# Attention and routed experts on one core: indices scattered a step later, statistics three tiles ahead, half of the W13 low parts made on TensorE, the last group ranked before the first gate

## The chip, the core and the metric

The kernel runs on one core of a Trainium2 chip. A core has TensorE (matmuls, result in PSUM banks of 512 fp32 columns), VectorE, ScalarE and GpSimd, which work beside each other and wait for each other by semaphores, and SyncE, which here only issues DMAs. The metric is the device time of one execution in microseconds.

## The reference

`x` is 4 x 512 x 512. The first layer adds a masked cross attention whose values are the normalised rows of x weighted element by element, the second a mixture of eight experts of which each token uses two.

```
xn = layernorm(x)                                     # (4, 512, 512)
scores = (ctx @ Wq.T + bq) @ (ctx @ Wk.T + bk).T * 128**-0.5 * xn
x = x + tanh(g_xattn) * softmax(where(mask, -inf, scores))
xn = layernorm(x)                                     # 2048 tokens of 512
w = sigmoid(xn @ Wg.T);  top 2 of 8 by w + bias, weights normalised to 1
x = x + tanh(g_ffn) * sum_e w_e * ((silu(xn @ W1[e].T) * (xn @ W3[e].T)) @ W2[e].T)
```

## The kernel before

**First half: 16 steps, one for each tile of 128 tokens.** Step s does the following for tile s, with parts of the neighbouring tiles between. TensorE computes the scores of the next tile (L889, fp32, two records in the trace) and its masks (L897, L898), transposes the normed rows of the tile before (L911) and computes the logits of the tile before that (L921). Every fourth step it projects q and k of the next batch (L882) into the banks `ps_q` and `ps_k`. In most steps it also runs twice three matmuls whose result nobody reads (`spin`, L904). VectorE multiplies scores with x (L658), takes the row maximum (L662), computes the bias of the exponential (L669), the statistics of the tile two further on (`first_stats`, L649 to L653) and, after the exponentials, the residual sum (L681). ScalarE takes the exponentials (L520), the sum of squares (L526), and copies the transposed rows (L535). GpSimd computes reciprocal square roots (`row_scales`, L389) and the normed rows (L404).

**Splitting the weights.** Matmuls of the experts run in fp32r; for precision each weight is split into a high part (a rounded copy) and a low part (weight minus high part). W13 comes in 16 units of 128x1024 (two for each expert), W2 in 8. In step s ScalarE makes the high parts of `SPLITS[s]` units (L558); the low part is made one step later by GpSimd for the units in `LO_BY_POOL` (L409) and by VectorE for the rest (L820). The low part is written over the weight as it was loaded. `LOADS` says in which step ScalarE issues the load of which weights.

**Routing.** Tiles are routed in groups of 6, 4 and 6. When a group's logits are there, VectorE ranks the experts of each token (`router_ranks`, L701 to L715), makes weights (`router_weights`, L724 to L735), and, when TensorE has counted positions (L931 to L940), the indices (`router_slots`, L750 to L762). GpSimd scatters each tile's entries, two DMAs for a tile, to a table of slots in DRAM (`enter_slots`, L416): `SCATTERS` gives for a step its group and the range of DMAs; the entries of group 0 begin in step 8, in which VectorE makes their indices. GpSimd works strictly in order: row scales, normed row, low parts, scatters. `list_tiles` makes the list of expert tiles: 13 entries after ten tiles are routed, the others after all 16.

**Second half: 39 list tiles.** For list tile i SyncE loads 128 slots (L334), GpSimd gathers their normed rows (L431, three buffers `xg`), TensorE transposes them (L959), ScalarE and VectorE split them (L572, L799), TensorE multiplies with W13 (`hidden`, L971 to L973), ScalarE and VectorE compute the gate (L580, L805, L808), TensorE transposes it (L983), VectorE splits it (L814, L816), TensorE multiplies with W2 (`output`, L999 to L1001), ScalarE scales the rows (L591) and GpSimd adds them to the output in DRAM (L450, an accumulating indirect DMA, called store below). Two buffers `y` hold the scaled rows. Stores 0 to 2 each wait until the one before has landed; later ones do so where `list_landed` asks for it, that is, where the expert changes. The 12 scatters of the last group stand between these stores (`LATE_SCATTERS`: before store i-1 in round i). The third gather waits for the logits of tile 15, because the columns they read lie in its buffer.

The order of all instructions is written out by hand in one program for each engine, and each engine works it off in order.

## Time and profile before

| | |
|---|---|
| median of 3 runs | 350.77 us (350.27 to 351.55) |
| the profiled execution | 353.24 us, its span in the trace 351.50 us |
| busy share of the span | TensorE 82%, VectorE 55%, ScalarE 36%, GpSimd 56% |
| bytes moved | 48.69 MB, mean 139 GB/s |
| median landing of an x tile's load | 4.4 us |
| median landing of a slot scatter | 7.4 us |
| chain that ended last, by engine | DMA 28%, issue 25%, GpSimd 17%, TensorE 15%, VectorE 10% |

The shares are means over two different halves: in the page's 40 slices of 8.8 us TensorE is at 9 tenths in nearly every slice from the 23rd on, while slices 7 to 15 vary. So it is read by stage, with the timeline: each row of it has the start, the duration, the engine and line, and in brackets how long the engine stood idle before it and what ended that.

### The profile page before, as it was taken

What the parts mean: (1) busy time and instruction counts of PE and PEld (TensorE: products, weight loads), DVE (VectorE), ACT (ScalarE), POOL (GpSimd) and SP (SyncE); (2) the same over time, 40 slices, a digit from 0 to 9 for tenths busy, and PEclk for the clock granted to TensorE, in tenths of its full rate; (3) what the DMA queues carried; (4) which work ended last, traced back from release to release, by engine and by line L of the source; (5) the groups of instructions that cost most, each with busy time, mean ns of one, the idle gap of its engine ahead of it and who ended that gap; (6) DMA issues with size and microseconds to landing.
All of it is one profiled execution on the core that took longest, in us unless ns stands there. A gap on an engine that the chain in (4) does not pass through costs nothing.

```text
span 351.5 us, 5188 instructions
## 1 busy us (share of the span) xinstructions
PE 289.7 (82%) x1324; PEld 210.3 (60%) x1330; DVE 193.0 (55%) x493; ACT 128.2 (36%) x239; POOL 197.7 (56%) x193
## 2 busy tenths in 40 slices
PE   3888985967787335898759899999999999999981
PEld 1244542534344224786547788888888888888860
DVE  3597989884999312775223445445545444544530
ACT  2677772644336322221113133332233333233320
POOL 4099794688568442237774555455545544754313
PEclk9999998588858558899969899999999999999996
DMA  7997978375884023335799556666556664865444
GB/s 203 334 408 269 340 234 340 122 174 91 282 200 90 3 61 101 110 62 60 50 74 118 79 105 121 103 122 108 109 100 121 122 98 84 144 107 113 58 61 60
DMA packets 27026, 48.69 MB, mean 139 GB/s; under 512 B 9524, under 2 KB 10296, under 8 KB 25976
## 3 DMA queue, kind: packets, MB, share of 16 engines
q0 software_dynamic: 9760, 20.49, 36.3%
q1 hardware_dynamic: 14408, 15.04, 14.3%
q10 hardware_dynamic: 2832, 12.85, 11.8%
q8 instruction: 13, 0.21, 0.3%
q14 instruction: 13, 0.11, 0.1%
HBM read 28.51 MB, written 19.85 MB: 138 GB/s over the span
## 4 chain that ended last, share of the span: by engine, by line
DMA 28%; issue 25%; POOL 17%; PE 15%; DVE 10%; POOLq 2%; ACT 2%; SPq 0%; ACTq 0%; DVEq 0%
DMA out<-rows,slot 23%; POOL slot_table L416 5%; POOL rows L431 5%; POOL out L450 3%; PE bank L882 3%; DMA rows<-xn_rows,slot 2%; PE bank L889 2%; PE bank L904 2%; PE bank L921 2%; DVE rows L681 1%; POOLq L442 1%; DMA w_hi<-in_ctx_t 1%; PE bank L911 1%; PE bank L959 1%; POOL rstds L389 1%
## 5 line engine op out<-in xcount | busy, mean ns | idle before, releaser
L450 POOL DMA_INDIRECT out<-rows,slot x39 | 62.2, 1596 | 77.0 <-DMA out<-rows,slot 33.8
L799 DVE TENSOR_TENSOR xt_lo<-bank,xt_hi 128x512 fp32r<-128x512 f32 x39 | 27.0, 691 | 75.9 <-ACT xt_hi L572 75.9
L971 PE MATMUL bank<-w_hi,xt_hi 128*128 x156 | 66.5, 427 | 0.0
L973 PE MATMUL bank<-w_hi,xt_lo 128*128 x156 | 62.3, 399 | 0.0
L972 PE MATMUL bank<-w_lo,xt_hi 128*128 x156 | 61.9, 397 | 0.0
L431 POOL DMA_INDIRECT rows<-xn_rows,slot x39 | 40.0, 1025 | 27.0 <-issue 16.8
L416 POOL DMA_INDIRECT slot_table<-entry,slot_index x32 | 35.4, 1105 | 24.3 <-DVE slot_index L762 16.0
L591 ACT ACTIVATE rows<-bank,slot 128x512 f32<-128x512 f32 x39 | 26.8, 687 | 60.8 <-PE bank L1001 38.1
L580 ACT ACTIVATE rows<-bank 128x256 f32<-128x256 f32 x39 | 15.0, 384 | 81.8 <-PE bank L973 81.8
L999 PE MATMUL bank<-w_hi,gt_hi 128*128 x78 | 31.3, 402 | 9.8 <-DVE gt_lo L816 9.8
L805 DVE SCALAR_TENSOR_TENSOR rows<-rows,bank 128x256 f32<-128x256 f32 x39 | 16.3, 419 | 37.9 <-ACT rows L580 37.8
L959 PE MATMUL bank<-ident,rows 128*128 128x128 f32 x156 | 25.7, 291 | 11.3 <-DMA rows<-xn_rows,slot 11.3
L973 PEld LDWEIGHTS bank<-w_hi,xt_lo 128*128 128x128 f32 x156 | 30.0, 192 | 7.0
L971 PEld LDWEIGHTS bank<-w_hi,xt_hi 128*128 128x128 f32 x156 | 30.6, 196 | 5.3 <-issue 0.4
L972 PEld LDWEIGHTS bank<-w_lo,xt_hi 128*128 128x128 f32 x156 | 30.6, 196 | 5.2
L1001 PE MATMUL bank<-w_hi,gt_lo 128*128 x78 | 31.2, 400 | 0.0
L1000 PE MATMUL bank<-w_lo,gt_hi 128*128 x78 | 30.8, 395 | 0.0
L959 PEld LDWEIGHTS bank<-ident,rows 128*128 128x128 f32 x156 | 20.9, 150 | 16.5 <-DMA rows<-xn_rows,slot 11.5
L904 PE MATMUL bank<-w_hi,ident_bf 128*128 128x512 bf16 x81 | 26.9, 449 | 2.9 <-ACT w_hi L515 2.6
L558 ACT CAST w_hi<-w_lo 128x1024 fp32r<-128x1024 f32 x24 | 24.3, 1036 | 9.7 <-DMA xn_rows<-w_hi 6.6
L572 ACT CAST xt_hi<-bank 128x512 fp32r<-128x512 f32 x39 | 22.6, 578 | 9.3 <-PE bank L959 9.3
L409 POOL TENSOR_TENSOR w_lo<-w_lo,w_hi 128x1024 fp32r<-128x1024 f32 x10 | 23.7, 2368 | 0.0
(128 smaller groups left out, 450.7 us busy)
## 6 DMA issues: line engine op xcount, KB each, us to landing
w_lo<-in_w ACTq DMA_DIRECT2D x8, 1024.0 KB, 6.8
xn_rows<-w_hi SPq DMA_DIRECT2D x17, 256.0 KB, 5.7
rows<-in_x SPq DMA_DIRECT2D x16, 256.0 KB, 4.4
out<-rows SPq DMA_DIRECT2D x16, 256.0 KB, 5.0
w_lo<-in_w ACTq DMA_DIRECT2D x8, 512.0 KB, 7.8
w_hi<-in_ctx_t SPq DMA_DIRECT2D x4, 256.0 KB, 4.3
slot<-slot_table SPq DMA_DIRECT2D x39, 1.0 KB, 1.7
rows<-xn_rows,slot POOLq DMA_INDIRECT x39, 4.2
```

Source lines behind the costliest of these rows:

```text
L416: pool.indirect_dma_start(out=table[:, :], out_offset=bass.IndirectOffsetOnAxis(ap=slot_index[:, g % 2, t, c:c + 1], axis=0), in_=entry[:, ...
L431: pool.indirect_dma_start(out=xg[:, i % XG, :], out_offset=None, in_=xn_rows[0:SPARE + P * READY[segment(i)], :], in_offset=bass.IndirectO ...
L450: pool.indirect_dma_start(out=out[0:SPARE + P * READY[segment(i)], :], out_offset=bass.IndirectOffsetOnAxis(ap=slot[:, i, 0:1].bitcast(U32 ...
L799: dve.tensor_tensor(xt_lo[:, i % 2].rearrange("p k s -> p (k s)"), ps_x[i % 2][:], xt_hi[:, i % 2].rearrange("p k s -> p (k s)").bitcast(F32),
L904: pe.matmul(ps_q[:], ident_bf[:], attn_neg[:, 0, :], start=True, stop=True)
L959: mm = pe.transpose(ps_x[i % 2][:, k * P:(k + 1) * P], xg[:, i % XG, k * P:(k + 1) * P], ident[:])
L971: pe.matmul(ps_h[i % 2][:], xt_hi[:, i % 2, k, :], hi, start=(k == 0), stop=False)
L972: pe.matmul(ps_h[i % 2][:], xt_hi[:, i % 2, k, :], lo, start=False, stop=False)
L973: mm = pe.matmul(ps_h[i % 2][:], xt_lo[:, i % 2, k, :], hi, start=False, stop=(k == KC - 1))
L999: pe.matmul(ps_o[i % 2][:], gt_hi[:, cols], hi, start=(c == 0), stop=False)
L1000: pe.matmul(ps_o[i % 2][:], gt_hi[:, cols], lo, start=False, stop=False)
L1001: mm = pe.matmul(ps_o[i % 2][:], gt_lo[:, cols], hi, start=False, stop=(c == FC - 1))
```

## The change

Numbers of lines are those of the kernel before. Seven things are changed.

- `LO_BY_PE`: in steps 3, 4, 6, 8, 9, 10, 11 and 12 TensorE makes the low part of one W13 unit: for each half of 512 columns, identity times the weight plus minus identity times the high part, into `ps_q` and `ps_k`; ScalarE copies both to the low part (`copy_lo`). VectorE makes no low part of W13 any more, GpSimd eight instead of ten, the last in step 8.
- `spin` runs five matmuls once a step instead of twice three, and not in the steps of `LO_BY_PE`.
- `SPLITS` and `LOADS` are shifted to fit.
- `SCATTERS` begins in step 9 and takes four DMAs in steps 13 and 14; `LATE_SCATTERS` begins in round 1, with two DMAs a round to round 5 and one in rounds 6 and 7.
- The first statistics of a tile, and its first row scale, come one step earlier, three tiles ahead.
- The columns of tile 15 lie in another row buffer, so the third gather does not wait for its logits. SyncE loads the first four slots before the store of tile 15's rows and the others behind it.
- In the second half the ranks of the last group stand before the first gate, its weights before the first split of the gate, its indices behind that. TensorE goes from hidden(0) through the last logits to hidden(1) and does the first gate's transposes behind it.

```diff
-    SPLITS = (1, 1, 2, 1, 2, 1, 2, 1, 2, 1, 2, 1, 1, 1, 1, 2)
-    LO_BY_POOL = (0, 1, 2, 4, 5, 7, 8, 10, 12, 14)
-    SCATTERS = {8: (0, 0, 3), 9: (0, 3, 6), 10: (0, 6, 9), 11: (0, 9, 12), 12: (1, 0, 2), 13: (1, 2, 5), 14: (1, 5, 8)}
-    LATE_SCATTERS = {2: (2, 0, 2), 3: (2, 2, 5), 4: (2, 5, 8), 5: (2, 8, 10), 6: (2, 10, 12)}
-    SPINS = 3
+    SPLITS = (1, 1, 2, 2, 1, 2, 1, 2, 1, 1, 1, 2, 1, 1, 1, 2)
+    LO_BY_POOL = (0, 1, 2, 4, 6, 7, 9, 10)
+    LO_BY_PE = {3: 3, 4: 5, 6: 8, 8: 11, 9: 12, 10: 13, 11: 14, 12: 15}
+    SCATTERS = {9: (0, 0, 3), 10: (0, 3, 6), 11: (0, 6, 9), 12: (0, 9, 12), 13: (1, 0, 4), 14: (1, 4, 8)}
+    LATE_SCATTERS = {1: (2, 0, 2), 2: (2, 2, 4), 3: (2, 4, 6), 4: (2, 6, 8), 5: (2, 8, 10), 6: (2, 10, 11), 7: (2, 11, 12)}
+    SPINS = 5
...
+            def subtract_high(step, projected):
+                unit = LO_BY_PE[step]
+                pe.wait_ge(s_hi, unit + 1)
                 pe.wait_ge(s_qk, 2 * projected)
+                pe.wait_ge(s_lo_act, 2 * sum(before_ < step for before_ in LO_BY_PE))
+                for c, bank_ in enumerate((ps_q, ps_k)):
+                    cols = slice(c * D, (c + 1) * D)
+                    pe.matmul(bank_[:], ident[:], raw(unit)[:, cols], start=True, stop=False)
+                    pe.matmul(bank_[:], minus_ident, high(unit)[:, cols], start=False, stop=True).then_inc(s_diff, 1)
...
+            def copy_lo(step):
+                for c, bank_ in enumerate((ps_q, ps_k)):
+                    n = 2 * sum(before_ < step for before_ in LO_BY_PE) + c
+                    act.wait_ge(s_diff, n + 1)
+                    act.copy(low(LO_BY_PE[step])[:, c * D:(c + 1) * D], bank_[:]).then_inc(s_lo_act, 1)
...
                 for unit in units_in(step):
                     split_hi(unit)
+                if step in LO_BY_PE:
+                    copy_lo(step)
                 squares(step)
...
                     row_done(TILES - XR + i)
-                    if i == 2:
-                        pool.wait_ge(s_logits, TILES)
...
-                if step + 2 < TILES:
-                    first_stats(step + 2)
+                if step + 3 < TILES:
+                    first_stats(step + 3)
...
             last = len(GROUPS) - 1
+            router_ranks(last)
             for i in range(LIST):
                 gate_rows(i)
                 if i + 2 < LIST:
                     gathered_lo(i + 2)
+                if i == 0:
+                    router_weights(last)
                 gated_transposed(i)
                 if i == 0:
-                    router_ranks(last)
+                    router_slots(last)
                 elif i == 1:
-                    router_weights(last)
-                elif i == 2:
-                    router_slots(last)
-                elif i == 3:
                     list_tiles(1)
...
                 if i == 0:
                     logits(TILES - 1)
+                    gathered(2)
+                elif i == 1:
+                    gate_transpose(0)
+                    positions(len(GROUPS) - 1)
+                    gathered(3)
+                    output(0, last)
+                    gate_transpose(1)
                 else:
                     output(i - 1, last)
-                if i + 2 < LIST:
-                    gathered(i + 2)
-                if i == 1:
-                    positions(len(GROUPS) - 1)
-                gate_transpose(i)
+                    if i + 2 < LIST:
+                        gathered(i + 2)
+                    gate_transpose(i)
```

TensorE before, in step 3, from the logits of tile 1 to those of tile 2: scores (L889), masks (L897, L898), spins (L904), transposes (L911), spins, logits (L921).

```order
L921 MATMUL bank<-wg_sb,w_hi 128x8 x4
L889 MATMUL bank<-w_hi 128x512
L897 MATMUL bank<-w_hi,ident_bf 128x512
L898 MATMUL bank<-w_hi,ident_bf 128x512
L904 MATMUL bank<-w_hi,ident_bf 128x512 x3
L911 MATMUL bank<-ident,w_hi 128x128 x4
L904 MATMUL bank<-w_hi,ident_bf 128x512 x3
L921 MATMUL bank<-wg_sb,w_hi 128x8 x4
```

TensorE in the changed kernel, same place. Scores are L912 there, the subtraction L931 and L932, masks L920 and L921, transposes L945, logits L955.

```order
L955 MATMUL bank<-wg_sb,w_hi 128x8 x4
L912 MATMUL bank<-w_hi 128x512
L931 MATMUL bank<-w_lo,ident 128x512
L932 MATMUL bank<-w_hi,gt_hi 128x512
L931 MATMUL bank<-w_lo,ident 128x512
L932 MATMUL bank<-w_hi,gt_hi 128x512
L920 MATMUL bank<-w_hi,ident_bf 128x512
L921 MATMUL bank<-w_hi,ident_bf 128x512
L945 MATMUL bank<-ident,w_hi 128x128 x4
L955 MATMUL bank<-wg_sb,w_hi 128x8 x4
```

Four matmuls on 512 columns stand where six spins were, and ahead of the masks.

GpSimd before, steps 8 and 9: row scales (L383, L389), normed row (L404), low part (L409), scatters (L416).

```order
L383 TENSOR_SCALAR variances<-sqsum 128x1
L389 TENSOR_TENSOR rstds<-variances,minus_half 128x2
L404 TENSOR_SCALAR w_hi<-rows,nmean,rstds 128x512
L409 TENSOR_TENSOR w_lo<-w_lo,w_hi 128x1024
L416 DMA slot_table<-entry,slot_index 19328x2 x3
L383 TENSOR_SCALAR variances<-sqsum 128x1
L389 TENSOR_TENSOR rstds<-variances,minus_half 128x2
L404 TENSOR_SCALAR w_hi<-rows,nmean,rstds 128x512
L409 TENSOR_TENSOR w_lo<-w_lo,w_hi 128x1024
L416 DMA slot_table<-entry,slot_index 19328x2 x3
```

GpSimd in the changed kernel, same steps, in its own line numbers (row scales L394 and L400, normed row L415, low part L420, scatters L427).

```order
L394 TENSOR_SCALAR variances<-sqsum 128x1
L400 TENSOR_TENSOR rstds<-variances,minus_half 128x2
L415 TENSOR_SCALAR w_hi<-rows,nmean,rstds 128x512
L420 TENSOR_TENSOR w_lo<-w_lo,w_hi 128x1024
L394 TENSOR_SCALAR variances<-sqsum 128x1
L400 TENSOR_TENSOR rstds<-variances,minus_half 128x2
L415 TENSOR_SCALAR w_hi<-rows,nmean,rstds 128x512
L427 DMA slot_table<-entry,slot_index 19328x2 x3
```

Step 8 has no scatters any more and step 9 no low part.

GpSimd at the start of the second half, before: gathers (L431), then in round 2 the first two late scatters (L416) before store 1 (L450).

```order
L431 DMA rows<-xn_rows,slot 128x512 x4
L450 DMA out<-rows,slot 1536x512
L431 DMA rows<-xn_rows,slot 128x512
L416 DMA slot_table<-entry,slot_index 19328x2 x2
L450 DMA out<-rows,slot 1536x512
L431 DMA rows<-xn_rows,slot 128x512
L416 DMA slot_table<-entry,slot_index 19328x2 x3
```

In the changed kernel (gathers L440, scatters L427, stores L459):

```order
L440 DMA rows<-xn_rows,slot 128x512 x4
L427 DMA slot_table<-entry,slot_index 19328x2 x2
L459 DMA out<-rows,slot 1536x512
L440 DMA rows<-xn_rows,slot 128x512
L427 DMA slot_table<-entry,slot_index 19328x2 x2
L459 DMA out<-rows,slot 1536x512
```

The first two scatters stand before store 0, and no round has three.

## Rows read from the trace of the kernel before

**Rows 1.** The page, part 2: granted TensorE clock in 40 slices, tenths

```profile
PEclk9999998588858558899969899999999999999996
```

**Rows 2.** Groups by line: busy us, mean ns, idle us before

```profile
L416 POOL DMA_INDIRECT slot_table<-entry,slot_index x32 | 35.4, 1105 | 24.3 <-DVE slot_index L762 16.0 <-issue 7.7 <-PE bank L959 0.6
...
L558 ACT CAST w_hi<-w_lo 128x1024 fp32r<-128x1024 f32 x24 | 24.3, 1036 | 9.7 <-DMA xn_rows<-w_hi 6.6 <-PE bank L921 2.0 <-PE bank L889 0.9
L409 POOL TENSOR_TENSOR w_lo<-w_lo,w_hi 128x1024 fp32r<-128x1024 f32 x10 | 23.7, 2368 | 0.0
...
L520 ACT ACTIVATE bank<-w_hi,nbias,rstds 128x512 f32<-128x512 f32 x16 | 12.5, 781 | 20.5 <-DVE nbias L669 19.7 <-issue 0.6
...
L526 ACT ACTIVATE bank<-rows,nmean 128x512 f32<-128x512 f32 x16 | 11.0, 688 | 7.8 <-DVE nmean L684 7.8
...
L535 ACT COPY w_hi<-bank 128x512 f32<-128x512 f32 x15 | 8.7, 580 | 14.7 <-PE bank L911 14.5
```

**Rows 3.** Timeline of TensorE, first half: start, duration, line, idle before

```profile
33.48 1.06 PE L921 MATMUL bank<-wg_sb,w_hi 128*128 128x8 f32 x8
34.40 1.10 PE L889 MATMUL bank<-w_hi 128*128 128x512 f32 x2
...
38.81 1.10 PE L889 MATMUL bank<-w_hi 128*128 128x512 f32 x2
...
54.45 1.10 PE L889 MATMUL bank<-w_hi 128*128 128x512 f32 x2
59.87 0.61 PE L897 MATMUL bank<-w_hi,ident_bf 128*128 128x512 bf16 x1 [4.32 <-DVE zmax L662]
...
66.31 2.05 PE L889 MATMUL bank<-w_hi 128*128 128x512 f32 x2
...
93.74 0.61 PE L897 MATMUL bank<-w_hi,ident_bf 128*128 128x512 bf16 x1 [1.96 <-DVE zmax L662]
...
100.71 2.05 PE L889 MATMUL bank<-w_hi 128*128 128x512 f32 x2
...
109.28 1.10 PE L889 MATMUL bank<-w_hi 128*128 128x512 f32 x2
```

**Rows 4.** Timeline of VectorE: after group 0's weights, and group 1's first rank instruction

```profile
58.35 0.74 DVE L658 SCALAR_TENSOR_TENSOR w_hi<-rows,mv,bank 128x512 f32<-128x512 f32 x1
...
86.88 1.47 DVE L701 TENSOR_SCALAR sig<-sig 128x32 f32<-128x32 f32 x1
```

**Rows 5.** Timeline of GpSimd: first and last scatter of the first half

```profile
63.43 1.25 POOL L416 DMA_INDIRECT slot_table<-entry,slot_index  x1 [6.68 <-DVE slot_index L762]
...
114.96 0.96 POOL L416 DMA_INDIRECT slot_table<-entry,slot_index  x1 [0.30 <-issue]
```

**Rows 6.** Timeline of all engines, 149 to 198 us

```profile
149.90 1.64 POOL L450 DMA_INDIRECT out<-rows,slot  x1 [5.41 <-issue]
...
153.98 0.47 PE L971 MATMUL bank<-w_hi,xt_hi 128*128 x1
...
158.74 0.47 PE L971 MATMUL bank<-w_hi,xt_hi 128*128 x1
...
160.16 1.61 POOL L450 DMA_INDIRECT out<-rows,slot  x1 [0.30 <-issue]
...
180.39 1.61 POOL L450 DMA_INDIRECT out<-rows,slot  x1 [0.30 <-issue]
...
197.32 0.78 PE L971 MATMUL bank<-w_hi,xt_hi 128*128 x1
```

**Rows 7.** Timeline of all engines, 120 to 145 us

```profile
122.65 13.97 SPq L334 DMA_DIRECT2D slot<-slot_table  x13
...
131.65 0.79 PE L971 MATMUL bank<-w_hi,xt_hi 128*128 x1
...
137.52 1.08 POOL L431 DMA_INDIRECT rows<-xn_rows,slot  x1 [8.05 <-PE bank L921]
...
141.68 1.12 PE L959 MATMUL bank<-ident,rows 128*128 128x128 f32 x4 [4.95 <-DMA rows<-xn_rows,slot]
```

**Rows 8.** The chain that ended last: start, us, what

```profile
167.55 8.65 DMA out<-rows,slot
...
337.71 4.69 DMA out<-rows,slot
```

74 lines of the change are left out of this document (47 added, 27 removed).

## The prediction, made before the changed kernel was run

> **What bounds the kernel now.** I read the page's clock row, then the timeline of TensorE, then of the engines it waits for. The kernel has two halves. In the first, 16 steps, one per tile of 128 tokens, do attention and normalisation; in the second, 39 list tiles go through the experts. From list tile 9 on TensorE is never idle and a tile takes 4.76 us (153.98 to 158.74) [rows 6]; nothing in the change alters a tile there, so the 154 us from its tile 9 (197.32) [rows 6] to the end move as a block. All that can move the end lies before 197.32.
>
> In the first half a plain step is TensorE's own: from one scores to the next 34.40 to 38.81, 4.41 us, with no wait [rows 3]. Then it breaks. At 59.87 TensorE has waited 4.32 us for VectorE's row maximum, because the ranks and weights of group 0 stood in front of it on VectorE until 58.35 [rows 3, 4]. After each such wait the clock row shows the lower level, 1.2 GHz [rows 1], and a scores matmul pair takes 2.05 us [rows 3] where 2 x 0.47 is usual. Then GpSimd binds: the first scatter waits 6.68 us for its indices, and from there to the last scatter's end (114.96 + 0.96 = 115.92) it is nearly all scatters, row scales, normed rows and low parts [rows 5]. Scores(9), (10), (14) and (15) come at 54.45, 66.31, 100.71 and 109.28 [rows 3]: six steps in 55 us.
>
> In the passage to the second half, SyncE starts the slot loads at 122.65, 6.7 us after the last scatter, the first expert matmul starts at 131.65, and then TensorE idles 4.95 us for the third gather, which GpSimd issued only at 137.52, after waiting for the last logits [rows 7]. From tile 0 to tile 9 it needs 65.7 us, where nine tiles at 4.76 would be 42.8: 22.8 us are lost, in the end to accumulating stores that queue behind each other and behind twelve late scatters [rows 6].
>
> **The change, part by part**, in the profiled execution's time (353.24, span 351.50; the median of the runs is 350.77, 2.47 less, and I carry the difference over).
>
> *Low parts on TensorE.* Eight of 16 W13 low parts become two pairs of matmuls into the q and k banks plus two ScalarE copies. No row has this operation whole, but its pieces have: an identity matmul on 512 fp32 columns is like scores, two records of 0.47 at the high clock, and one in fp32r is 0.23, since a tile has 18 of them in its 4.76 us beside 0.6 of transposes. So 2 x (0.94 + 0.23) = 2.3 us on TensorE, and 2 x 0.58 on ScalarE (a copy of 128x512 from a bank takes 580 ns [rows 2]). It is not hidden by either engine, since the two form a ring: logits 0.92 (33.48 to 34.40), scores 0.94, subtraction 2.3, second copy 0.68 with its wait, squares 0.69 + 0.19, copy of the transposed rows 0.58, semaphores 0.25 in all, and the next logits wait for that copy. 6.5 us, against 4.41 [rows 2, 3]. From below, TensorE's own work in such a step is 5.3 us (no spins); from above, the same ring at 1.2 GHz is 0.92 + 0.94 + 2.3 more, 10.7. I take 6.5.
> What goes: six VectorE subtractions and, net, two GpSimd ones of 2.37 [rows 2].
>
> *Spins.* Six a step become five, and none in a low-part step: a plain step keeps its 4.4, since ScalarE with two units has 0.97 + 2 x 1.0 + 0.88 + 0.58 = 4.4 [rows 2]. In project steps nothing stands any more behind the wait for ScalarE's bias: 1.2 us less in step 2.
>
> Steps 2 to 7: step 2 -1.2, steps 3 and 4 +2.1 each, step 6 (low part and projection, about 7.1 against 6.8) +0.3: **+3.3**.
>
> *Step 8*, scores(9) to scores(10), 54.45 to 66.31, 11.9 us. Ranks end as before, 3.9 us after scores(9); then maximum and bias 1.7, exponentials 0.97, high part 1.04, two copies 1.2, squares 0.9, transposed copy 0.6, logits 0.95, waits 0.3: 11.4. **-0.5**. The low part fills most of the old 4.3 us wait, but the chain now runs over ScalarE.
>
> *Scatters a step later, statistics a tile earlier.* GpSimd no longer stands before normed rows waiting for indices, and the row scale of a tile no longer comes from behind that step's scatters. With no low part left in steps 9 to 14 its step is row scales and normed row 2.1 and three scatters 3.9 (1.1 each, 1.28 with the gap [rows 2]), 6.0: under the ring's 6.5. So steps 9 and 10 take 6.5 and 7.1; steps 11 and 12, with the ranks of group 1 between (4.1: the old 5.3, less the 1.3 by which their first instruction, 1.47 instead of 0.18, waited beside a GpSimd low part [rows 4]), 13.7; step 13 4.6. Scores(10) to scores(15): 31.9, before 109.28 - 66.31 = 43.0. **-11.1**. Behind that steps 13 and 14 have four scatters, and the last one ends 8.3 us after scores(15), before 6.6: **+1.7**. What is late next is ScalarE's chain, then GpSimd's four-scatter steps.
> The statistics ask for each x tile a step sooner. Tile 6 is issued at 24.36 and would be wanted about 27.6, with 4.4 us as the median landing: up to 1.2 us or, with the slowest landing (6.5), 3.3 of VectorE's waiting in step 3, and as much in steps 4, 6 and 7. The longer low-part steps cover it (+2.1 each); I count 0, at most 3.
>
> *Clock.* TensorE will still idle some 2 us in front of the maximum of step 8 and 3 more behind its transposes. Idle spells of 4.32 and 1.96 us were followed by the low level [rows 3, 1]; spells of about 1 us in the early steps were not. Bounds: 0, or one ring step and the rest of step 8 low, 4.2 + 0.7. I take **+2**.
>
> *SP.* One normed store goes ahead of the first slot load: **+0.4**. The first half so yields 3.3 - 0.5 - 11.1 + 1.7 + 2 + 0.4 = **-4.2** at the first expert matmul: 127.4.
>
> *Second half, up to tile 9* (in the old times, tile 0 at 131.65). The third gather needs no last logits and lands before 135, so tile 1 starts near 137.2 instead of 142.87. But VectorE now does the 3.2 us of ranks before the first gate, 137.0 to 140.2, then gate 0.9, weights 1.8, split 0.8: output(0) waits until 144.4, and tile 3 comes at 152.0 instead of 153.98. What matters is the stores: indices at 145.2 instead of 157.3, two scatters, store 0 at 148.0 (149.90), store 1 after store 0's landing (6.6 to 8.7 us [rows 8]) at 155 to 157 (160.16), store 2 at 162 to 165 (167.55). Then GpSimd's round is gather 1.3, two scatters 2.6, store 1.9: 5.8 instead of 7.1; store 4 at 174 to 177 (180.39). Tile 9 followed it by 16.9 us: 191 to 194 [rows 6]. **-6**, bounds -2 (only the two us at tile 3) and -12 (landing as fast as the later 4.7).
>
> Sum: 353.24 - 4.2 - 6 = 343.0, in the runs' terms 350.77 - 10.2 = **340.5**.
>
> On the stores the rows show landings of 8.65 us amid scatters and 4.69 later [rows 8]. The Trainium skill, "DMA: Bandwidth & Descriptors", section "Issuing engines are not separate DMA queues", says that all issuers share 16 engines and interleave; it goes against the gain, since spreading twelve scatters over seven rounds instead of five puts more stores beside them. By it the last term would be nearer its -2, and the sum 344.5.
>
> **Rivals.**
> 1. *The clock stays low through the ring* (slower). TensorE idles 1.2 us in every low-part step. At 1.2 GHz the ring gains 4.2 us a step. If steps 8 to 12 are all low, that is 5 x 4.2 = 21, less the 2 counted: 350.77 - 10.2 + 19 = 359.5. It decides from three such steps on (3 x 4.2 - 2 = 10.6). For it: after 59.87 and 93.74 the clock stayed low some 13 us [rows 1, 3]. Against it: TensorE works 5.3 us of 6.5, and in the first 50 us waits of 1.0 left the clock up. The Trainium skill's "TensorE: Matmul & The Clock Gate", section "A second HAM failure mode: psum-queue depth-cycling", tells of frequent short idles that make the clock oscillate; the ring would be such a case, and no row before shows it.
> 2. *The stores keep the second half* (less gain). Tile 9 waits for store landings; if these lengthen with gathers and scatters closer together, the six us there are nil and only the first half counts: 350.77 - 4.2 = 346.5. For it: 33.8 us of GpSimd's waits are on stores. Against it: the chain begins earlier in any case.
> 3. *Both run well* (more gain): no clock loss (-2), landings of 6.6 (-5): 333.5. For it: the low part fills the very idle time after which the clock fell.
>
> **How the numbers follow.** Forecast 0.52, rival 2 0.20, rival 3 0.17, rival 1 0.11. 0.5% or 1.75 us is about what a measurement tells from no change. Slower by more: rival 1's larger part, 0.09, and 0.01 of mishaps; within: 0.06, from rival 2's upper end (x tiles late, +3) and rival 1 with two low steps; faster: 0.84. The range leaves rival 1 and the best fifth of rival 3 out: 331.5 to 350. The likeliest's own is 336 to 345.
>
> **What would show it.** Low-part steps of 6.5 us between scores in steps 3, 4, 9 and 10; no wait of GpSimd for indices in step 9; the last scatter of the first half ending near 111; first expert matmul near 127; no gap before tile 1 but one of about 3 us before output(0); store 4 some 42 to 45 us after tile 0 instead of 48.7 (180.39 - 131.65). I am wrong if scores lie over 9 us apart in steps 9 and 10 (clock or x tiles), or if tile 9 still comes 65 us after tile 0.

## The result, and the profile after

The changed kernel takes **349.37 us** (median of 20 runs, 343.74 to 353.38), the kernel before 351.19 in the same series (20 runs, 348.71 to 353.74). The ratio is **0.9887, interval 0.9852 to 0.9923**, faster by 1.1% or 4 us, where 10 were forecast. Ratios and intervals in this document use only the executions within 1.5% of their kernel's fastest, which are all 20 of the kernel before but 7 of the 20 of the changed one, so its ratio flatters it: the medians of all executions lie 1.8 us or 0.5% apart (0.9948). The profiled execution took 348.12 us, its span is 346.4.

| stretch, profiled executions | forecast | before | after | difference |
|---|---|---|---|---|
| start to scores(9) | +3.3 | 54.45 | 59.00 | +4.6 |
| scores(9) to scores(10) | -0.5 | 11.86 | 12.00 | +0.1 |
| scores(10) to scores(15) | -11.1, clock +2 | 42.97 | 40.18 | -2.8 |
| scores(15) to the end of the last scatter | +1.7 | 6.64 | 8.98 | +2.3 |
| from there to the first expert matmul | +0.4 | 15.73 | 15.58 | -0.2 |
| **first expert matmul** | **-4.2** | 131.65 | 135.74 | **+4.1** |
| tile 0 to tile 9 | -6 | 65.67 | 57.20 | -8.5 |
| tile 9 to the end of the span | 0 | 154.18 | 153.46 | -0.7 |

The sum, -5.1, is the difference of the two profiled executions (353.24 and 348.12). The first is 2.05 us above its kernel's median and the second 1.25 below, so some 3 us of the table are a matter of which executions were profiled.

The groups by line, answering to [rows 2], with the new subtraction (L931) and copies (L609):

```profile
L427 POOL DMA_INDIRECT slot_table<-entry,slot_index x32 | 33.7, 1052 | 21.8 <-issue 14.7 <-DVE slot_index L781 6.9 <-ACT rows L603 0.3
...
L420 POOL TENSOR_TENSOR w_lo<-w_lo,w_hi 128x1024 fp32r<-128x1024 f32 x8 | 18.9, 2358 | 0.0
...
L931 PE MATMUL bank<-w_lo,ident 128*128 128x512 f32 x32 | 18.4, 660 | 0.0
...
L609 ACT CAST w_lo<-bank 128x512 fp32r<-128x512 f32 x16 | 9.2, 585 | 10.8 <-PE bank L932 10.8
```

Scatters wait less for indices than before, but 14.7 us "issue", for nothing that the profile can name. That is the new item. A copy takes 585 ns, as forecast. The records of the subtraction's identity matmul (two for each) average 660 ns; some ran at the low clock.

TensorE, first half, answering to [rows 3], with the page's clock row:

```profile
59.00 1.10 PE L912 MATMUL bank<-w_hi 128*128 128x512 f32 x2
...
71.00 2.05 PE L912 MATMUL bank<-w_hi 128*128 128x512 f32 x2
...
79.30 1.10 PE L912 MATMUL bank<-w_hi 128*128 128x512 f32 x2
...
86.22 1.13 PE L912 MATMUL bank<-w_hi 128*128 128x512 f32 x2
...
92.36 1.81 PE L912 MATMUL bank<-w_hi 128*128 128x512 f32 x2
...
100.31 1.10 PE L912 MATMUL bank<-w_hi 128*128 128x512 f32 x2
...
104.53 0.61 PE L920 MATMUL bank<-w_hi,ident_bf 128*128 128x512 bf16 x1 [3.12 <-DVE zmax L681]
...
109.45 1.88 PE L955 MATMUL bank<-wg_sb,w_hi 128*128 128x8 f32 x8 [0.68 <-ACT w_hi L545]
...
111.18 2.05 PE L912 MATMUL bank<-w_hi 128*128 128x512 f32 x2
```

```profile
PEclk9998999769885555889998999999999999999997
```

```profile
66.00:74.00 8.00, 6.09 (x31) 4.14 (x29) 6.55 (x23) 5.06 (x11) 4.02 (x6) 0.50 0.60 197
```

Scores(10) at 71.00, scores(11) at 79.30: 8.3 us instead of the 6.5 forecast, since the clock stood at 1.2 GHz from 66 to 74 us (0.50 in the row of the window above: busy us of TensorE, its weight loads, VectorE, ScalarE, GpSimd, then the clock); the next steps take 6.9, 6.1 and 8.0. Then, from 100.31 to 111.18, one step takes **10.9** where 4.6 was forecast. TensorE waits 3.12 us for VectorE's maximum, its clock falls to 1.2 GHz in that time, and its logits take 1.88 us instead of 1.06 and its scores 2.05. There is one more fall, at the start of the low-part step 12: the scores at 92.36 took 1.81 us, and no wait of TensorE since 79 us had been over 0.78 us. The granted clock, in the last column but two:

```profile
79.00:92.00 13.00, 12.22 (x49) 6.62 (x50) 8.23 (x31) 9.84 (x20) 9.29 (x13) 1.00 0.86 150
93.00:95.50 2.50, 2.50 (x5) 1.01 (x3) 2.43 (x5) 0.98 (x3) 2.02 (x3) 0.50 1.32 316
```

VectorE in that step: first and last instruction of `list_tiles(0)`, and what stands behind them.

```profile
99.21 0.26 DVE L787 TENSOR_REDUCE n_tiles<-compared 1x8 f32<-1x128 f32 x1
...
102.81 0.15 DVE L813 TENSOR_TENSOR used<-used,taken 1x7 f32<-1x7 f32 x1
...
103.00 0.75 DVE L677 SCALAR_TENSOR_TENSOR w_hi<-rows,mv,bank 128x512 f32<-128x512 f32 x1
...
103.78 0.69 DVE L681 CUSTOM_DVE_ANT_0 w_hi<-w_hi,bank 128x512 f32<-128x512 f32 x1
```

The list of expert tiles takes 3.8 us (99.21 to 102.96) in sixteen tiny instructions, and only then comes the product whose maximum TensorE waits for. The forecast had counted ranks and weights of group 1 but not this list.

GpSimd, answering to [rows 5]: second, third and last scatter of group 1.

```profile
102.49 0.96 POOL L427 DMA_INDIRECT slot_table<-entry,slot_index  x1 [0.30 <-issue]
...
110.05 0.97 POOL L427 DMA_INDIRECT slot_table<-entry,slot_index  x1 [6.60 <-issue]
...
118.82 1.34 POOL L427 DMA_INDIRECT slot_table<-entry,slot_index  x1 [0.30 <-issue]
```

Between two scatters of one step GpSimd stands for 6.60 us, and no engine and no DMA is named. Normed rows, TensorE's transposes of them and the last scatter all come behind that: the last scatter ends at 120.16, before at 115.92.

The second half, answering to [rows 6, 7] (SyncE's queue, TensorE and GpSimd):

```profile
135.74 0.79 PE L1005 MATMUL bank<-w_hi,xt_hi 128*128 x1
...
149.27 0.49 PE L1032 MATMUL bank<-w_hi,gt_hi 128*128 x1 [1.84 <-DVE gt_lo L837]
...
150.75 1.00 POOL L427 DMA_INDIRECT slot_table<-entry,slot_index  x1 [6.87 <-DVE slot_index L781]
...
153.34 1.63 POOL L459 DMA_INDIRECT out<-rows,slot  x1 [0.30 <-issue]
...
160.28 1.61 POOL L459 DMA_INDIRECT out<-rows,slot  x1 [1.43 <-DMA out<-rows,slot]
...
178.60 1.61 POOL L459 DMA_INDIRECT out<-rows,slot  x1 [0.30 <-issue]
...
192.94 0.48 PE L1005 MATMUL bank<-w_hi,xt_hi 128*128 x1
```

Here the forecast holds. There is no gap before tile 1 any more, and before output(0) TensorE waits 1.21 and 1.84 us, where one gap of 3 was forecast. Counted from tile 0, the first late scatter starts at 15.0 us (forecast 13.6, before 25.9), store 0 comes at 17.6 (before 18.3), store 1 at 24.5 (before 28.5), store 4 at 42.9 (before 48.7; forecast 42 to 45), tile 9 at 57.2.

### The profile page after: what moved, and what is told of

The parts are those of the page before. It is cut to its first block, busy times and chain, and to the rows that moved or that the text cites. A ratio compares the mean times of both kernels' runs of the same rounds, so it can differ in the third digit from the quotient of the medians.

```text
span 346.4 us, 5203 instructions
## 1 busy us (share of the span) xinstructions
PE 294.9 (85%) x1320; PEld 213.1 (62%) x1324; DVE 183.8 (53%) x488; ACT 135.5 (39%) x255; POOL 184.6 (53%) x192
## 3 DMA queue, kind: packets, MB, share of 16 engines
q10 hardware_dynamic: 2832, 12.85, 13.6%
## 4 chain that ended last, share of the span: by engine, by line
DMA 36%; issue 24%; PE 16%; POOL 11%; DVE 6%; ACT 4%; POOLq 2%; ACTq 0%; SPq 0%; DVEq 0%
DMA out<-rows,slot 29%; POOL rows L440 4%; DMA xn_rows<-w_hi 4%; PE bank L912 3%; POOL out L459 3%; PE bank L931 3%; POOL slot_table L427 3%; PE bank L955 3%; PE bank L905 2%; ACT bank L536 1%; DMA rows<-xn_rows,slot 1%; DMA w_hi<-in_ctx_t 1%; POOLq L451 1%; PE bank L938 1%; DMA slot_table<-entry,slot_index 1%
## 5 line engine op out<-in xcount | busy, mean ns | idle before, releaser
L459 POOL DMA_INDIRECT out<-rows,slot x39 | 62.0, 1591 | 70.7 <-DMA out<-rows,slot 36.8
L1007 PE MATMUL bank<-w_hi,xt_lo 128*128 x156 | 62.2, 399 | 0.0
L440 POOL DMA_INDIRECT rows<-xn_rows,slot x39 | 39.0, 1001 | 24.0 <-issue 16.7
L427 POOL DMA_INDIRECT slot_table<-entry,slot_index x32 | 33.7, 1052 | 21.8 <-issue 14.7
L993 PE MATMUL bank<-ident,rows 128*128 128x128 f32 x156 | 24.9, 284 | 6.7 <-DMA rows<-xn_rows,slot 6.7
L955 PE MATMUL bank<-wg_sb,w_hi 128*128 128x8 f32 x120 | 18.8, 284 | 10.2 <-ACT w_hi L545 10.2
L993 PEld LDWEIGHTS bank<-ident,rows 128*128 128x128 f32 x156 | 20.1, 146 | 11.9 <-DMA rows<-xn_rows,slot 7.2
L955 PEld LDWEIGHTS bank<-wg_sb,w_hi 128*128 128x128 f32 x120 | 18.0, 228 | 15.1 <-ACT w_hi L545 13.7
```

The source lines that it names most:

```text
L427: pool.indirect_dma_start(out=table[:, :], out_offset=bass.IndirectOffsetOnAxis(ap=slot_index[:, g % 2, t, c:c + 1], axis=0), in_=entry[:, ...
L440: pool.indirect_dma_start(out=xg[:, i % XG, :], out_offset=None, in_=xn_rows[0:SPARE + P * READY[segment(i)], :], in_offset=bass.IndirectO ...
L459: pool.indirect_dma_start(out=out[0:SPARE + P * READY[segment(i)], :], out_offset=bass.IndirectOffsetOnAxis(ap=slot[:, i, 0:1].bitcast(U32 ...
L955: mm = pe.matmul(ps_l[:, t * E:(t + 1) * E], normed_columns(tile)[:, k, :], wg_sb[:, k, :], start=(k == 0), stop=(k == KC - 1))
L993: mm = pe.transpose(ps_x[i % 2][:, k * P:(k + 1) * P], xg[:, i % XG, k * P:(k + 1) * P], ident[:])
L1007: mm = pe.matmul(ps_h[i % 2][:], xt_lo[:, i % 2, k, :], hi, start=False, stop=(k == KC - 1))
```

## The experiments

Twelve runs were made to find which part gains and which costs, six more on the wait that has no name. Each ratio is to the kernel before, run on the same chip in the same series; the series are on different chips, so a comparison of two kernels goes by their ratios and not by their times. Tile 0 stands for the first expert matmul.

| kernel | ratio [interval] | unnamed wait of a scatter, us | last scatter ends | tile 0 |
|---|---|---|---|---|
| changed | 0.9887 [0.9852, 0.9923] | 6.60, at the 15th | 120.2 | 135.7 |
| e1 room halved (two executions) | 1.0223 [1.0182, 1.0264] | 11.06 at the 8th, 4.22 at the 15th, 3.98 at the 20th | 129.8 | 143.4 |
| e2 list later | 0.9896 [0.9843, 0.9949] | 3.60, 15th | 121.1 | 137.1 |
| e3 second half only | 0.9839 [0.9801, 0.9876] | none | 115.6 | 131.3 |
| e4 first half only | 1.0196 [1.0168, 1.0225] | 3.32, 15th | 118.4 | 133.2 |
| e5 without TensorE's low parts | 0.9867 [0.9811, 0.9924] | 7.66, 15th | 119.1 | 133.6 |
| e6 e3 + statistics | 0.9787 [0.9731, 0.9843] | none | 117.4 | 133.1 |
| e7 e3 + new SCATTERS | 0.9821 [0.9753, 0.9889] | 8.55, 15th | 122.6 | 137.5 |
| e8 e3 + TensorE's low parts | 0.9768 [0.9719, 0.9817] | none | 119.8 | 135.4 |
| e9 changed, old SCATTERS | **0.9784 [0.9744, 0.9823]** | none | 117.9 | 133.2 |
| e10 three a step | 0.9935 [0.9891, 0.9978] | 5.36, 15th | 124.3 | 140.0 |
| e11 e9 + list later | **0.9764 [0.9726, 0.9802]** | none | 120.8 | 136.7 |
| e12 e3, old late scatters | 0.9859 [0.9813, 0.9905] | none | 115.8 | 132.3 |
| e13 e9, W2 loads earlier | 0.9827 [0.9785, 0.9868] | none | 118.4 | 134.8 |
| e14 small x1 stores | 0.9866 [0.9803, 0.9928] | 8.47, 15th | 123.1 | 137.8 |
| e15 W2 loads earlier | 0.9953 [0.9907, 0.9998] | 7.03, 15th | 123.0 | 138.1 |
| e16 room for twelve | 0.9934 [0.9889, 0.9978] | 6.57, at the 13th | 122.7 | 138.0 |
| e17 e9, room for twelve | 0.9846 [0.9801, 0.9892] | 8.21, at the 13th | 118.5 | 133.5 |
| e18 two first | 1.0027 [0.9996, 1.0058] | none | 124.2 | 140.0 |

The last three columns are from one execution each. Executions of one kernel differ by 2.8% or more (343.74 to 353.38 for the changed one), so a tile 0 that is 2 us off says little by itself; the ratios decide.

**e1, room for descriptors.**

```diff
-SCRATCH = 2048
+SCRATCH = 1024
```

> The changed kernel with the descriptor buffer of GpSimd's DMAs halved (1024 instead of 2048). In step 13 GpSimd stood 6.6 us between its second and third scatter with no releaser in the trace. Theory R (room for descriptors): it waited for older scatters to give their room back; with half the room such waits come at many scatters, gathers and stores and the kernel is slower by 10 us or more. Rival (the wait has another cause, and room is not short): the time stays within 1 us of the changed kernel's, 349.

```profile
98.69 0.97 POOL L427 DMA_INDIRECT slot_table<-entry,slot_index  x1 [11.06 <-issue]
```

The wait grows to 11.06 us and two more appear; 1.0223 is 3.4% over the changed kernel's ratio (2.7% by the medians of all executions), from two executions. The unnamed wait has to do with the room for GpSimd's descriptors: nothing else was changed.

**e2, the list out of step 13.**

```diff
-                    if END[g] in READY:
-                        list_tiles(READY.index(END[g]))
...
+            list_tiles(0)
             for unit in units_in(TILES - 1):
                 split_lo(unit)
```

> The changed kernel, with the list of the first 13 expert tiles made by VectorE after the last residual sum instead of in step 12, where its 3.7 us stand before the row maximum of tile 13. Theory V (VectorE): that block idles TensorE 3.1 us, the clock falls and step 13 takes 10.9 us; without it scores(14) to scores(15) take 5 to 6 us, the first half ends 3 to 5 us earlier, and the time is 345 to 346. Rival G (GpSimd): its 6.6 us wait in step 13 sets the end of the scatters by itself; step 13 gets shorter on TensorE but the last scatter still ends near 120 and the time stays at 349.

The step becomes 6.9 us instead of 10.9, and the time stays (0.9896). So TensorE's and VectorE's loss in step 13 isn't what the end waits for; in the profile the last scatter still ends at 121.1, with an unnamed wait of 3.60 us before it.

**e3 and e4, one half each.** e3 has the first half of the kernel before and the second of the changed one, e4 the reverse.

```diff
-    LO_BY_PE = {3: 3, 4: 5, 6: 8, 8: 11, 9: 12, 10: 13, 11: 14, 12: 15}
+    LO_BY_PE = {}
...
-    SCATTERS = {9: (0, 0, 3), 10: (0, 3, 6), 11: (0, 6, 9), 12: (0, 9, 12), 13: (1, 0, 4), 14: (1, 4, 8)}
+    SCATTERS = {8: (0, 0, 3), 9: (0, 3, 6), 10: (0, 6, 9), 11: (0, 9, 12), 12: (1, 0, 2), 13: (1, 2, 5), 14: (1, 5, 8)}
...
-            row_scales(-2)
...
-            first_stats(2)
```

> Only the second half of the change on the kernel before (ranks of the last group ahead of the first gate, late scatters from round 1, third gather without the last logits, slot loads split); the first half as before. Theory A (the halves add up): the first expert matmul stays near 131.7, tile 9 comes 57 us later, and the time is 342 to 343, 9 below the kernel before. Rival: the second half's gain needs the changed first half (DMAs of the first half landed by then), and the time is 346 to 349.

> Only the first half of the change (low parts on TensorE, scatters a step later, statistics three ahead), the second half as before. Theory A: the first expert matmul is at 135 to 136 and the time is 355, 4 above the kernel before. Rival: with the old second half the later start is partly taken up by its waits for stores, and the time is 351 to 352.

The second half alone brings 1.6%, or 5.6 us of 351, the six forecast. The first half alone costs 2.0%, or 6.9 us, where a gain of 4.2 was forecast. They don't add up to the changed kernel's -1.1%; the rest (about 5 us, or 2 to 3 by the medians of all executions) is not accounted for.

**e5 to e8, the first half's parts.** e5 is the changed kernel without TensorE's low parts; e6, e7 and e8 add to e3 the earlier statistics, the new SCATTERS, and TensorE's low parts (with `SPLITS`, `LOADS` and spins). As e3 against e7:

```diff
-    SCATTERS = {8: (0, 0, 3), 9: (0, 3, 6), 10: (0, 6, 9), 11: (0, 9, 12), 12: (1, 0, 2), 13: (1, 2, 5), 14: (1, 5, 8)}
+    SCATTERS = {9: (0, 0, 3), 10: (0, 3, 6), 11: (0, 6, 9), 12: (0, 9, 12), 13: (1, 0, 4), 14: (1, 4, 8)}
```

> The changed kernel without the low parts on TensorE: units, loads and spins of the first half as in the kernel before, but scatters from step 9 and statistics three tiles ahead, and the new second half. The new second half alone ran at 0.984 of the kernel before, the whole change at 0.989, the first half alone at 1.020. Theory P (the low parts on TensorE cost what is lost, by steps of 6.1 us and the ring over ScalarE): this runs at 0.975 to 0.985. Rival S (twenty scatters in six steps run out of descriptor room): it still waits for room in steps 12 to 14 and runs at 0.99 or more.

> The new second half alone plus statistics and row scales three tiles ahead. Theory P and rival S both expect the same as without it, 0.984, since the bias of the exponentials waited for row scales only 1.0 us in the kernel before; a third theory X (VectorE waits for x tiles that land late, as it does for 1.9 us in the changed kernel) expects 2 us more, 0.990.

> The new second half alone plus scatters from step 9, four each in steps 13 and 14. Rival S: waits without a releaser at the later scatters, the last one ends later than 115 and the time is 0.99 to 1.00. Theory P: GpSimd no longer stands 6.7 us before the first scatter, the last one ends earlier or at the same time, 0.975 to 0.985.

> The new second half alone plus the low parts on TensorE (with their units, loads and spins), scatters from step 8 as before. Theory P: low-part steps of 6.1 us instead of 4.4 put off the first scatters by 3 us and more, and the time is 0.99 to 1.00. Rival S: the low parts cost nothing at the end, since GpSimd's scatters bind as before, and with four GpSimd low parts fewer the time is 0.98.

TensorE's low parts show no cost in the time: 0.9768 against e3's 0.9839, though low-part steps take 6.1 us. Nor do the statistics (0.9787). So far the unnamed wait is in each kernel with the new SCATTERS and in none with the old. In the time this shows in one pair, 0.9867 (e5) against 0.9787 (e6), whose intervals still overlap, and not in the other (e7 against e3). So one run more:

**e9, the changed kernel with the old SCATTERS; e10, three a step; e11, e9 with the list later; e12, the spacing of the late scatters.**

```diff
+    SCATTERS = {8: (0, 0, 3), 9: (0, 3, 6), 10: (0, 6, 9), 11: (0, 9, 12), 12: (1, 0, 2), 13: (1, 2, 5), 14: (1, 5, 8)}      e9, e11
+    SCATTERS = {9: (0, 0, 3), 10: (0, 3, 6), 11: (0, 6, 9), 12: (0, 9, 12), 13: (1, 0, 3), 14: (1, 3, 6), 15: (1, 6, 8)}     e10
+    LATE_SCATTERS = {2: (2, 0, 2), 3: (2, 2, 5), 4: (2, 5, 8), 5: (2, 8, 10), 6: (2, 10, 12)}                               e12, on e3
```

> The changed kernel with one line back as it was: SCATTERS starts in step 8 and has three DMAs a step, two in step 12. Theory S (the new SCATTERS takes back what the rest gains): about 344 us, 0.977 of the kernel before, no wait without a releaser over 1 us among GpSimd's scatters, last scatter of the first half ending at 117 to 119. Theory A (low parts on TensorE and statistics three ahead lose only together, whatever the scatters do): 349 us as the changed kernel, 0.989, list tile 0 at 135 or later.

> The changed kernel with the scatters of group 1 spread as three, three and two over steps 13, 14 and 15, so the start in step 9 stays and no step has four. Theory F (the four in a row fill the room for descriptors): the wait of 6.6 us in step 13 shrinks to under 2, the last scatter ends at 117 to 119, about 346 us (0.983). Theory L (the later start does it, since as many descriptors must be moved in a shorter stretch beside the loads of W2): the wait of 4 to 8 us stays, somewhere in steps 12 to 15, last scatter at 120 or later, about 349 us (0.989).

> The changed kernel with the old SCATTERS and the first list of expert tiles behind the last residual, out of step 13. If VectorE's 3.8 us there count once GpSimd no longer binds: 341 us (0.971), 3 us under the same kernel with the list in its place. Rival G (GpSimd's scatters and row scales set the end of the first half in this form too): no difference from it, within 1 us of 344.

> The kernel with only the second half changed (344.67 us, 0.984) with the old spacing of the last group's scatters: from round 2, three a round in rounds 3 and 4. Theory D (the stores come sooner because fewer scatters stand between them): half of the gain goes, 347.5 us, 0.992, and list tile 9 comes 58 us after tile 0 instead of 54. Rival T (only the earlier ranks, indices and third gather count): within 1 us of 344.7, tile 9 at 54 to 55 us.

With the one line back, the ratio is 0.9784, its interval clear of the changed kernel's: the new SCATTERS costs 1.0%, or 3.6 us (1.6% by the medians of all executions). Three a step doesn't cure it (0.9935, wait 5.36): so it isn't the fours, and the later start is what is left. The list's place is again worth nothing that shows (e11 against e9). For e12 the answer stays open: 0.9859 against 0.9839 with overlapping intervals, though in its one profile tile 9 came 62.2 us after tile 0 instead of 54.0.

GpSimd in e9, the fourteenth and fifteenth scatter, and VectorE's subtraction beside the fifteenth:

```profile
103.87 0.96 POOL L427 DMA_INDIRECT slot_table<-entry,slot_index  x1 [0.30 <-issue]
...
107.13 1.22 DVE L841 TENSOR_TENSOR w_lo<-w_lo,w_hi 128x1024 fp32r<-128x1024 f32 x1
...
107.21 2.07 POOL L427 DMA_INDIRECT slot_table<-entry,slot_index  x1 [0.28 <-issue]
```

Row scales and a normed row stand between the two, so the fifteenth comes 3.3 us after the fourteenth without an unnamed wait. It takes 2.07 us instead of 0.96 to 1.09, but that is no sign of the room. A VectorE subtraction on 128x1024 (L841) had started 0.08 us before it, and every first-half scatter over 1.7 us in e9, the changed kernel and the kernel before stands beside such a subtraction: the 11th of the changed kernel (1.81 us), the 2nd, 4th, 15th and 19th of the kernel before (1.75 to 2.07). In e11 the fifteenth takes 1.06 and the fourteenth, with the subtraction beside it, 1.92.

**e13 to e15, is it the traffic?** Loads of W2 one step earlier, in e9 (e13) and in the changed kernel (e15); in e14 the stores of x1 are cut from tile 8 on, as its expectation says, so it leaves out 448 of 512 columns of these rows, and only its waits and its time are read.

```diff
-    LOADS = {..., 7: (7,), 8: (8,), 9: (9,), 10: (10, 11), 11: (12, 13), 12: (14, 15)}
+    LOADS = {..., 7: (7, 8), 8: (9,), 9: (10, 11), 10: (12, 13), 11: (14, 15)}                    e13, e15
...
-                sp.dma_start(out[SPARE + tile * P:SPARE + (tile + 1) * P, :], x_row(tile))
+                cols = D if tile < 8 else D // 8
+                sp.dma_start(out[SPARE + tile * P:SPARE + (tile + 1) * P, 0:cols], x_row(tile)[:, 0:cols])      e14
```

> The changed kernel with the old SCATTERS (345.34 us, 0.978) and the loads of W2 one step earlier each (steps 7 to 11 instead of 8 to 12). If the loads beside group 1's scatters still cost something there: 342 us (0.970) and the last scatter a us or two before 117.9. If not, or if the bytes only collide earlier with the stores of steps 8 and 9: 345 us (0.978), within 1.5 us.

> The changed kernel with the stores of x1 from tile 8 on cut to their first 64 of 512 columns (the rest of these rows isn't written; as many descriptors, 1.8 MB less to move, about 1.1 of them between 85 and 120 us). Theory T (bytes in flight beside the scatters delay their descriptors, so that the room stays full): the wait without a releaser in step 13 falls from 6.6 us to under 3, W2 loads land in under 12 us instead of 14. Theory N (only the number of descriptors and when they are issued counts): the wait stays at 5 to 8 us and the time within 1.5 us of the changed kernel's 349.4.

> The changed kernel, new SCATTERS included, with the loads of W2 one step earlier each. Theory T: two of the W2 loads no longer stand beside group 1's scatters, the wait of 6.6 us in step 13 falls to under 4 us, about 347 us (0.983). Theory N: the wait stays at 5 to 8 us and the time at 349.4 (0.989).

The wait is 8.47 us with 1.8 MB less to move and 7.03 with the loads moved. Theory T fell; both kernels with earlier loads are slower, if anything (e13 0.9827 against e9's 0.9784, e15 0.9953 against 0.9887).

**e16 to e18, the end of the ring.** In e18 group 1's scatters come as two, three and three.

```diff
-SCRATCH = 2048
+SCRATCH = 1792                                                                            e16, e17 (on e9)
...
+    SCATTERS = {..., 12: (0, 9, 12), 13: (1, 0, 2), 14: (1, 2, 5), 15: (1, 5, 8)}         e18
```

> The changed kernel with the room for descriptors at 1792 bytes instead of 2048. The long wait stood at the fifteenth scatter with 2048 and at the eighth with 1024, so a scatter takes between 137 and 146 bytes and twelve fit in 1792. Theory W (the room is a ring; the first scatter that doesn't fit in it waits until the ones before it have landed): the wait moves to the thirteenth scatter, the first of step 13, 3 to 7 us long, and the fifteenth has none; the last scatter comes 1 to 3 us sooner than 118.8, 347.5 us (0.985). Theory U (room for so many in flight, less room is worse): still a wait at the third and fourth scatter of step 13 as well, over 8 us in all, 352 us (1.00).

> The changed kernel with the old SCATTERS (345.34 us, 0.978) and room for twelve scatters. Theory W: the thirteenth scatter waits for its indices until 102.5 in any case, so the end of the ring costs nothing there, no wait without a releaser over 1 us comes up, and the fifteenth takes about 1.0 us instead of 2.07; last scatter 1 us sooner than 116.9, 344 us (0.975). Theory U: waits of some us at the thirteenth to eighteenth scatter, 348 us (0.987).

> The changed kernel with group 1's scatters as two, three and three in steps 13, 14 and 15, room as it was. Theory W: the fifteenth scatter is now the first of step 14 and stands behind its row scales and normed row, so the long wait stands there and is 1 to 4 us instead of 6.6 (5.36 with three, three and two); last scatter at 120 or later, since three come in step 15; 348 to 351 us. Theory U: no wait over 1 us, since never more than three are issued in a row.

GpSimd in e16, the twelfth, thirteenth and fifteenth scatter:

```profile
97.38 0.96 POOL L427 DMA_INDIRECT slot_table<-entry,slot_index  x1 [0.30 <-issue]
...
108.09 1.07 POOL L427 DMA_INDIRECT slot_table<-entry,slot_index  x1 [6.57 <-issue]
...
111.69 0.96 POOL L427 DMA_INDIRECT slot_table<-entry,slot_index  x1 [0.30 <-issue]
```

The wait has moved to the thirteenth, as theory W said, and the fifteenth has none. So the room is used up in order, like a ring: fourteen scatters fit in 2048 bytes, twelve in 1792, seven in 1024, and the one after them waits though the first ones landed long before.

What ends the wait can be read from the landings. The changed kernel's twelfth scatter (start 96.75, the last of group 0) and its fourteenth (102.49):

```profile
L427 POOL DMA_INDIRECT slot_table<-entry,slot_index x1: 958/958/958, 96.7 to 96.7; - x1
DMA to landing us min/median/max: 12.7/12.7/12.7
...
L427 POOL DMA_INDIRECT slot_table<-entry,slot_index x1: 958/958/958, 102.5 to 102.5; - x1
DMA to landing us min/median/max: 9.8/9.8/9.8
```

The twelfth landed at 109.4, and the fifteenth started 0.6 us later, at 110.05. The fourteenth landed at 112.3, after that: so the fifteenth doesn't wait for the one ahead of it. The same 0.6 to 0.7 us lie between the twelfth's landing and the fifteenth's start in e2 (110.6, 111.27), e4 (108.2, 108.92), e14 (111.3, 111.94) and e15 (111.8, 112.46), while over all kernels whose fifteenth waits with 2048 bytes it starts anything from 4.3 us (e4) to 9.9 (e7) after the scatter ahead. In e1 the eighth starts at 98.69 and the seventh landed at 98.1. In e16 the last landing of group 0 that the trace records is at 107.4, and the thirteenth starts at 108.09. Why it is the twelfth, of fourteen in the room, stays open.

This tells why starting a step sooner helps: in the kernel before the twelfth had landed at 101.8, 1.7 us before the fifteenth came up (103.55), and in e9 the last recorded landing of group 0 is at 102.4 and the fifteenth comes up at 107.2. What W said of the time fell: in e16 the last scatter ends at 122.7, no sooner, and 0.9934 isn't better than the changed kernel. The end of the wait is the same landing, and eight scatters instead of six are behind it. In e18 the fifteenth scatter, now behind a step's row scales, starts at 112.22 and has no wait at all, and yet that kernel is the slowest of all but e1 and e4: its scatters go on into step 15 and end at 124.2. e17's 8.21 us lie where e9 waits 5.99 for the indices, so most of them are that wait under another name (its thirteenth starts at 102.84, e9's at 102.48); its last scatter ends at 118.5, not sooner than e9's, and theory W's 344 us were 345.9. Moving the ring's end gave nothing; starting a step sooner did.

## Why the prediction was wrong

The first half's term failed: -4.2 us at the first expert matmul were forecast, +4.1 were measured in the profile, and the first half alone (e4) costs 2.0%. The forecast counted twenty scatters as engine time only and saw no wait behind them, and it left the list of expert tiles out of step 13. The second half's term held. Of the stretch forecast at -11.1 (scores(10) to scores(15), measured -2.8), step 13 missed 6.3 us and step 9 missed 1.8.

- **Low parts on TensorE.** Forecast 6.5 us for such a step, measured 6.1 at the high clock (30.23 to 36.31). To scores(9) +4.6 instead of +3.3. Mechanism right, and by e8 no cost of it shows in the time. The miss is beside the low-part steps: the 1.2 us of step 2 were not gained, since its five spins ran at the low clock (0.50 from 24.5 to 27.7 us, 2.31 us instead of 1.25), and the plain steps 5 and 7 took 4.9 us instead of 4.4.

```profile
24.40 2.31 PE L938 MATMUL bank<-w_hi,ident_bf 128*128 128x512 bf16 x5
```

- **Step 8, forecast -0.5, measured +0.1.** The terms written out for it add up to 11.6 us and not 11.4; measured 12.0.
- **The clock.** A low stretch behind the wait of step 8 was forecast at +2; step 9 took 8.3 instead of 6.5, +1.8. Three more weren't: in step 2, at 92.36 and in step 13. Rival 1, the low clock through the whole ring, didn't happen: steps 10 and 11 took 6.9 and 6.1. Behind that rival stood the Trainium skill's "TensorE: Matmul & The Clock Gate", section "A second HAM failure mode: psum-queue depth-cycling". In steps 3 and 4 the trace shows no such oscillation (1.00 from 29 to 60 us); the short fall at 92.36, behind low-part steps with waits of at most 0.8 us, may be of the kind that it tells of, and step 12, which begins with it, took 8.0 us.
- **Step 13, forecast 4.6, measured 10.9.** This is the largest error of a single step. "The ranks of group 1 between" were priced at 4.1; the 3.8 us of `list_tiles(0)` behind them were left out. In the kernel before the same list stood at the same place (VectorE, 98.45 to 101.78), and TensorE waited only 1.13 us for the maximum behind it. As soon as GpSimd's work was taken away, the next engine's own row had to be priced, and it wasn't. With the low clock behind it this makes the 6.3 us that step 13 missed. e2 shows that mending this alone gives nothing in the time.

```profile
103.89 0.60 PE L898 MATMUL bank<-w_hi,ident_bf 4*128 4x512 bf16 x1 [1.13 <-DVE zmax L662]
```

- **"Steps 13 and 14 have four scatters": +1.7, measured +2.3.** The price per scatter was right, the path wrong, and this is the step of the argument that the time turns on. The last scatter was to end near 111 and ended at 120.2. The end of the first half is the path from group 1's indices over eight scatters to the slot loads. From the first to the end of the last of these scatters before took 17.1 us (98.81 to 115.92), after 19.1 (101.10 to 120.16) with 6.6 of wait in it, e9 15.4 (102.48 to 117.88). The forecast counted scatters as engine time only. Their descriptors need room, and the fifteenth starts only after the landing of the twelfth. In the kernel before that landing came 1.7 us before the fifteenth scatter did, so the wait was just missed, and a later start brings it out. GpSimd's rows of the kernel before, the twelfth scatter with its landing (91.17 + 10.6 = 101.8) and the fifteenth:

```profile
L416 POOL DMA_INDIRECT slot_table<-entry,slot_index x1: 958/958/958, 91.2 to 91.2; - x1
DMA to landing us min/median/max: 10.6/10.6/10.6
...
103.55 2.07 POOL L416 DMA_INDIRECT slot_table<-entry,slot_index  x1 [0.28 <-issue]
```

- **Starting a step later.** The forecast took the wait of 6.68 us [rows 5] as lost, and its removal as a gain. But the first steps didn't gain from its removal what was forecast: scores(14) came at 100.31 instead of 100.71 before, where 98.4 was forecast with the clock's +2, and the indices of group 1 were ready no sooner (VectorE's last instruction for them ends at 99.3, before at 98.5). The later start puts the landing of group 0's scatters 7.6 us later (109.4 instead of 101.8), into the path that counts. e9 puts it at 1.0% of the time. With that mended the first half still has no gain: tile 0 comes at 133.2 in e9 and, with the list moved too, at 136.7 in e11. That part of the miss is laid to the clock and to step 2 from the trace alone; no run tests it.
- **Statistics three ahead** cost nothing, as counted.
- **Second half, forecast -6 (-2 to -12).** Measured -8.5 in the profile and 1.6% (5.6 us) by e3. Tile 3 gained nothing (22.3 us after tile 0, as before), against the 2 forecast; stores 1, 2 and 4 came within the ranges given. Tile 9 followed store 4 by 14.3 us instead of 16.9, and that is the 2.5 us more. Why is not shown: two scatters stand between stores 4 and 7 in either kernel, before both ahead of store 5, now one ahead of each of stores 5 and 6. The forecast's own store times gave tile 9 at 191 to 194, that is -3.3 to -6.3; the -6 taken was the good end of them. Rival 2 fell with the gain: stores 0 to 3 landed in 6.1, 5.9, 6.9 and 8.7 us, with two scatters ahead of each, and the first two in less than the 6.6 to 8.7 assumed. The Trainium skill's "DMA: Bandwidth & Descriptors", by whose section "Issuing engines are not separate DMA queues" the term would have been near -2, doesn't size it here.

The range of 331.5 to 350 held the 349.37 by 0.6 us, and faster was right by sign. Both are luck as far as the first half goes: the second half's gain outweighed a loss that nothing in the forecast allowed for. Nor did the two signs of being wrong show it (9 us between scores in steps 9 and 10, tile 9 at 65 us after tile 0); the last scatter, named at 111, did.

The lowest ratios are e11 (0.9764), e8 (0.9768), e9 (0.9784) and e6 (0.9787), and they can't be told apart. e3, with nothing of the first half's change, has 0.9839, and its interval overlaps those of e6, e8 and e9. So no part of the first half's change has a gain that is shown, and the first expert matmul came at 131.3 us in e3 and at 133.1 or later in the others, where the kernel before had 131.65: the 4.2 us forecast there appear in no profile.

## What to carry to other kernels

When a bound engine is relieved, price every instruction of the next one in that stretch, those too that cost nothing so far; a helper of sixteen tiny instructions is 3.8 us here. An indirect DMA needs room for its descriptors as well as time on its engine: a wait that the profile can give to nothing, at the same ordinal in each variant, was the end of that room here, and changing the room moved it. Compare the start behind such a wait with the landings of earlier DMAs: that names the one it waits for. A wait at the front of a long series of transfers may be free while the series' end is what counts; starting the series later to remove it moves the end.

## What the hardware showed that was not expected

With 2048 bytes of room the fifteenth scatter waits 3.3 to 8.6 us where group 0's twelve haven't landed when it comes up, with 1792 bytes the thirteenth, with 1024 the eighth; it starts 0.5 to 0.7 us after the landing of the twelfth (with 1024 bytes: of the seventh). In the changed kernel the thirteenth and fourteenth were still in flight then (landed at 111.8 and 112.3, start 110.05). Halving the room cost 3.4%, from two executions.

A scatter issued while VectorE was at a 128x1024 subtraction took 1.75 to 2.07 us of GpSimd instead of 0.96 to 1.09 (2nd, 4th, 15th and 19th of the kernel before).

In the loaded stretch one store of normed rows took 13.94 us to land:

```profile
86.06 13.94 DMA xn_rows<-w_hi
```

The clock fell to 1.2 GHz during an idle time of 3.12 us (it was 1.00 from 101.4 to 102.8 us and 0.50 from 103.0 to 104.5; the idle time ended at 104.53). It also fell at about 92.6 us with no wait over 0.78 us in the 13 us before. In the earlier low-part steps, where TensorE stands for 0.7 us ahead of each logits, it was 1.00 from 29 to 60 us:

```profile
29.00:60.00 31.00, 27.86 (x123) 15.63 (x124) 20.13 (x65) 23.45 (x44) 19.20 (x21) 1.00 0.85 268
```
